# Edge loop of a graph layer: the split of the edge attributes leaves GpSimd for ScalarE and VectorE, and the messages' remainder becomes VectorE's

## The reference

```
x: (1250, 512)   src, dst: (20000,)   edge_attr: (20000, 64)      all float32
edge_feat = concat([x[src], x[dst], edge_attr])        # (20000, 1088)
h         = mish(edge_feat @ W1 + b1)                  # mish(v) = v * tanh(softplus(v))
messages  = mish(h @ W2 + b2)                          # (20000, 512)
agg       = segment_sum(messages, dst)                 # (1250, 512)
u = mish(concat([x, agg]) @ W3 + b3);  y = x + u @ W4 + b4;  layernorm;  then experts
```

## Time and profile before

| | |
|---|---|
| median of 3 runs | 1414.67 us (1414.13 to 1416.09) |
| the profiled execution | 1416.24 us, of it span 1414.6 us |
| busy share of the span | PE 81%, PEld 64%, DVE 78%, ACT 60%, POOL 65% |
| mean granted TensorE clock | 0.933 |
| DMA | 148 MB, mean 105 GB/s |

### The profile page before, as it was taken

One profiled execution on the slowest core, in us unless ns is written; L12 is line 12 of the kernel. 1 busy time (PEld: TensorE's weight loads), 2 busy tenths in 40 slices (PEclk: granted clock), 3 DMA queues, 4 the chain that ended last, 5 costly groups with the idle time before them and its releaser, 6 DMA issues. The chain is left out here.

```text
span 1414.6 us, 20672 instructions
## 1 busy us (share of the span) xinstructions
PE 1145.5 (81%) x5823; PEld 912.1 (64%) x5824; DVE 1108.9 (78%) x1627; ACT 852.9 (60%) x1061; POOL 913.7 (65%) x755
## 2 busy tenths in 40 slices
PE   0992888889889899899898889889838997559972
PEld 0671666777677677677677777767626775558861
DVE  3840579999999999999999999999864876743364
ACT  1311667777777777777777777777843543333341
POOL 1333788898888888889889889888431210454410
PEclk9996899999999999999999999999968997679965
DMA  5534554554554554455455455455210111634452
GB/s 145 200 116 98 117 107 96 109 114 96 107 111 101 102 111 106 98 111 110 98 109 112 96 110 113 96 106 108 81 38 23 37 44 44 189 106 131 127 164 101
DMA packets 113398, 148.00 MB, mean 105 GB/s; under 512 B 55389, under 2 KB 63980, under 8 KB 113225
## 3 DMA queue, kind: packets, MB, share of 16 engines
q0 software_dynamic: 40912, 101.69, 32.8%
q1 hardware_dynamic: 72377, 45.20, 11.6%
q10 hardware_dynamic: 16, 0.02, 0.0%
HBM read 136.29 MB, written 15.66 MB: 107 GB/s over the span
## 5 line engine op out<-in xcount | busy, mean ns | idle before, releaser
L696 POOL DMA_INDIRECT gath<-dst_table,idx_sl x166 | 283.8, 1709 | 49.7 <-issue 27.2
L828 PE MATMUL ps<-W2l,hTh 128*128 128x512 f32 x664 | 264.2, 398 | 0.0
L828 PE MATMUL ps<-W2h,hTh 128*128 128x512 f32 x664 | 263.5, 397 | 0.0
L721 POOL TENSOR_TENSOR msg_lo<-act,msg_hi 128x1024 fp32r<-128x1024 f32 x83 | 213.3, 2570 | 33.9 <-DVE msg_hi L800 33.9
L706 POOL DMA_INDIRECT gath<-src_table,idx_sl x166 | 171.6, 1034 | 76.7 <-issue 50.3
L806 DVE TENSOR_TENSOR dloc<-idx_sl,block_off 128x2 f32<-128x2 int32 x83 | 180.3, 2172 | 14.9 <-DMA idx_sl<-idx_scr 14.9
L828 PE MATMUL ps<-W2h,hTl 128*128 128x512 f32 x664 | 174.9, 405 | 0.4 <-DVE hTl L795 0.2
L828 PEld LDWEIGHTS ps<-W2l,hTh 128*128 128x128 f32 x664 | 125.7, 189 | 30.6
L828 PEld LDWEIGHTS ps<-W2h,hTh 128*128 128x128 f32 x664 | 126.0, 190 | 26.4
L793 DVE TENSOR_TENSOR agg<-agg,ps 125x512 f32 x166 | 112.9, 680 | 31.0 <-DVE agg L793 23.3
L746 ACT ACTIVATE act<-act 128x1024 f32<-128x1024 f32 x83 | 88.2, 1062 | 77.6 <-DVE act L782 77.6
(11 more groups left out here) (315 smaller groups left out, 2852.2 us busy)
## 6 DMA issues: line engine op xcount, KB each, us to landing
f_w_raw<-in_L_ffn_w_dram SPq DMA_DIRECT2D x32, 512.0 KB, 4.6
ea_sl<-ea_scr SPq DMA_DIRECT2D x166, 32.0 KB
ea_scr<-in_edge_attr_dram POOLq DMA_DIRECT2D x1, 5000.0 KB, 20.6
w_raw<-in_L_gnn_W_dram SPq DMA_DIRECT2D x3, 1024.0 KB, 18.6
idx_sl<-idx_scr SPq DMA_DIRECT2D x166, 1.5 KB, 1.7
gath<-src_table,idx_sl POOLq DMA_INDIRECT x166, 4.2
gath<-dst_table,idx_sl POOLq DMA_INDIRECT x166, 5.2
x_raw<-in_x_dram SPq DMA_DIRECT2D x5, 500.0 KB
```

The lines of the kernel that those rows point to most:

```text
L696: pool.indirect_dma_start(out=gath[:, k, j, :], out_offset=None, in_=dst_table[:, :], in_offset=bass.IndirectOffsetOnAxis(ap=idx_sl[:, b % ...
L721: nc.gpsimd.tensor_tensor(msg_lo[:, m % 2], act2[:, m % 3], f32(msg_hi[:, m % 2]), ALU.subtract).then_inc(S["msg_lo_ready"], 1)
L828: return nc.tensor.matmul(ps_2[:, r % 2, j, :], part[:, r % 2, d, j * P:(j + 1) * P], weights[:, d, :], start=False, stop=last)
```

## The change

The attributes are no longer split by POOL. SP loads them twice, into both halves of a tile `ea_sl` that is 128 wide; PE transposes it, so that the 64 attributes stand in PSUM twice, on partitions 0 to 63 and 64 to 127. ACT copies all of it out rounded. A new instruction on DVE then replaces the upper half by what the rounding left (`eaT_lo`, 64 partitions by 256). The messages' remainder `msg_lo` is made by DVE. POOL's loop holds only the gathers.

The order on three engines changes with it. DVE: `hTl`, `msg_hi` and `msg_lo` stand ahead of the additions to `agg`, and `dloc` and `onehot` stand at the end of the step. ACT: the copy of the attributes stands behind both logarithms (it stood between them). PE: four of the eight lo passes stand ahead of the attributes' transposes, and the transposes of `gath` begin with the two blocks that lie in the other PSUM bank.

```diff
-        ea_sl = sb("ea_sl", [P, IN, 2, EDIM])
-        ea_hl = sb("ea_hl", [P, 2, 2, 2 * EDIM], F32R)
+        ea_sl = sb("ea_sl", [P, IN, 2, 2 * EDIM])
...
-                        sp.wait_ge(S["split"], q - IN + 1)
+                        sp.wait_ge(S["eaT_ps"], q - IN + 1)
...
-                        sp.dma_start(ea_sl[:, k, j, :], ea_scr[bass.ds(first, P), :]).then_inc(ea_in[k], 16)
+                        for half in range(2):
+                            sp.dma_start(ea_sl[:, k, j, half * EDIM:(half + 1) * EDIM], ea_scr[bass.ds(first, P), :]).then_inc(ea_in[k], 16)
...
-                    nc.gpsimd.tensor_copy(ea_hl[:, k, :, 0:EDIM], ea_sl[:, b % IN]).then_inc(S["ea_hi"], 1)
-                    pool.wait_ge(S["ea_hi"], b + 1)
-                    nc.gpsimd.tensor_tensor(ea_hl[:, k, :, EDIM:2 * EDIM], ea_sl[:, b % IN], f32(ea_hl[:, k, :, 0:EDIM]), ALU.subtract).then_inc(S["split"], 1)
...
-                    nc.gpsimd.tensor_tensor(msg_lo[:, m % 2], act2[:, m % 3], f32(msg_hi[:, m % 2]), ALU.subtract).then_inc(S["msg_lo_ready"], 1)
...
+                    nc.scalar.activation(a2, a2, ACT.Ln, bias=half_col[:], scale=0.5).then_inc(S["ln2"], 1)
                 if exists(n):
                     act.wait_ge(S["eaT_ps"], n + 1)
...
-                    nc.scalar.activation(eaT[:, n % 2, :], ps_1[:, n % 2, 0, :], ACT.Copy).then_inc(S["eaT_ready"], 1)
-                if second:
-                    act.wait_ge(S["sq2"], g + 1)
-                    nc.scalar.activation(a2, a2, ACT.Ln, bias=half_col[:], scale=0.5).then_inc(S["ln2"], 1)
+                    nc.scalar.activation(eaT[:, n % 2, :], ps_1[:, n % 2, 0, :], ACT.Copy).then_inc(S["eaT_hi"], 1)
...
+                    nc.vector.tensor_copy(msg_hi[:, m % 2], act2[:, m % 3]).then_inc(S["msg_hi_ready"], 1)
+                    dve.wait_ge(S["msg_hi_ready"], m + 1)
+                    nc.vector.tensor_tensor(msg_lo[:, m % 2], act2[:, m % 3], f32(msg_hi[:, m % 2]), ALU.subtract).then_inc(S["msg_lo_ready"], 1)
...
+                t = s + 1
+                if exists(t):
+                    dve.wait_ge(S["eaT_hi"], t + 1)
+                    nc.vector.tensor_tensor(eaT[EDIM:, t % 2, :], ps_1[EDIM:, t % 2, 0, :], f32(eaT[EDIM:, t % 2, :]), ALU.subtract).then_inc(S["eaT_lo"], 1)
...
                     nc.vector.scalar_tensor_tensor(out=act2[:, g % 3], in0=act2[:, g % 3], scalar=1.0, in1=ps_2[:, g % 2],
                                                    op0=ALU.subtract, op1=ALU.mult).then_inc(S["msg_ready"], 1)
+                if exists(n):
+                    dve.wait_ge(*loaded(idx_in, IN, n, 32))
+                    nc.vector.tensor_tensor(dloc[:, 2 * n:2 * n + 2], idx_sl[:, n % IN, :, 2], block_off[:, 2 * n:2 * n + 2], ALU.subtract).then_inc(S["dst_ready"], 1)
+                if exists(m):
+                    dve.wait_ge(S["dst_ready"], m + 1)
+                    nc.vector.tensor_tensor(onehot[:, m % 2], iota_n[:].unsqueeze(1).to_broadcast([P, 2, NE]),
+                                            dloc[:, 2 * m:2 * m + 2].unsqueeze(2).to_broadcast([P, 2, NE]), ALU.is_equal).then_inc(S["onehot_ready"], 1)
...
+                if exists(r):
+                    pe.wait_ge(S["h_lo"], r + 1)
+                    lo_tile(0)
...
-                    pe.wait_ge(S["split"], n + 1)
+                    pe.wait_ge(*loaded(ea_in, IN, n, 64))
...
-                        ins = nc.tensor.transpose(ps_1[:, k, 0, j * P:(j + 1) * P], f32(ea_hl[:, k, j, :]), ident[:])
+                        ins = nc.tensor.transpose(ps_1[:, k, 0, j * P:(j + 1) * P], ea_sl[:, n % IN, j, :], ident[:])
...
+                    lo_tile(1).then_inc(S["lin2_ps"], 1)
...
+                    for d in (2, 3, 0, 1):
+                        if d == 0:
+                            pe.wait_ge(S["eaT_lo"], n + 1)
```

More of the change, by code:

```diff
@@ L648, in edge_phase @@
         src_gath, both_gath = slots("src_gath", GA), slots("both_gath", GA)
-        names = ("ea_hi split dst_ready eaT_ps eaT_ready gath_read lin1_ps exp1 inc1 sq1 ln1 quot1 h_ready h_hi h_lo lin2_ps "
+        names = ("dst_ready eaT_ps eaT_hi eaT_lo gath_read lin1_ps exp1 inc1 sq1 ln1 quot1 h_ready h_hi h_lo lin2_ps "
                  "exp2 inc2 sq2 ln2 quot2 msg_ready msg_hi_ready msg_lo_ready onehot_ready sum_ps summed w3_in w3_hi w3_lo").split()
@@ L752, in _ @@
                     nc.scalar.activation(a1, a1, ACT.Ln, bias=half_col[:], scale=0.5).then_inc(S["ln1"], 1)
+                if second:
+                    act.wait_ge(S["sq2"], g + 1)
+                    nc.scalar.activation(a2, a2, ACT.Ln, bias=half_col[:], scale=0.5).then_inc(S["ln2"], 1)
                 if exists(n):
@@ L785, in _ @@
                     nc.vector.tensor_scalar(act2[:, g % 3], act2[:, g % 3], EXP_MAX, 1.0, ALU.min, ALU.add).then_inc(S["inc2"], 1)
+                if exists(r):
+                    nc.vector.tensor_tensor(hTl[:, r % 2], act1[:, r % 2], f32(hTh[:, r % 2]), ALU.subtract).then_inc(S["h_lo"], 1)
+                if exists(m):
+                    if m >= 2:
+                        dve.wait_ge(S["sum_ps"], m - 1)
+                    dve.wait_ge(S["msg_ready"], m + 1)
+                    nc.vector.tensor_copy(msg_hi[:, m % 2], act2[:, m % 3]).then_inc(S["msg_hi_ready"], 1)
+                    dve.wait_ge(S["msg_hi_ready"], m + 1)
+                    nc.vector.tensor_tensor(msg_lo[:, m % 2], act2[:, m % 3], f32(msg_hi[:, m % 2]), ALU.subtract).then_inc(S["msg_lo_ready"], 1)
                 if exists(a):
@@ L850, in _, with lo_tile @@
                     hi_tile(1)
+                def lo_tile(j):
+                    for d in range(KC):
+                        ins = lin2(j, d, hTl, W2h, d == KC - 1)
+                    return ins
+                if exists(r):
+                    pe.wait_ge(S["h_lo"], r + 1)
+                    lo_tile(0)
                 if exists(n):
                     k = n % 2
-                    pe.wait_ge(S["split"], n + 1)
+                    pe.wait_ge(*loaded(ea_in, IN, n, 64))
                     if n >= 2:
@@ L856, in _ @@
                     if n >= 5:
-                        pe.wait_ge(S["summed"], (n - 4) * 2)
+                        pe.wait_ge(S["summed"], (n - 5) * 2 + 1)
                     for j in range(2):
-                        ins = nc.tensor.transpose(ps_1[:, k, 0, j * P:(j + 1) * P], f32(ea_hl[:, k, j, :]), ident[:])
+                        ins = nc.tensor.transpose(ps_1[:, k, 0, j * P:(j + 1) * P], ea_sl[:, n % IN, j, :], ident[:])
                     ins.then_inc(S["eaT_ps"], 1)
                 if exists(r):
[L862 to L866, removed]
+                    lo_tile(1).then_inc(S["lin2_ps"], 1)
                 if exists(n):
                     k = n % 2
-                    pe.wait_ge(S["eaT_ready"], n + 1)
                     pe.wait_ge(*loaded(both_gath, GA, n, 32))
-                    for d in range(KC):
+                    if n >= 5:
+                        pe.wait_ge(S["summed"], (n - 4) * 2)
+                    for d in (2, 3, 0, 1):
+                        if d == 0:
+                            pe.wait_ge(S["eaT_lo"], n + 1)
                         for j in range(2):
```

10 lines of the change are left out of this document (removed).

## The result

| | before | changed |
|---|---|---|
| median | 1414.40 us | 1568.28 us (1565.02 to 1571.62) |
| ratio | | 1.1085, 95% interval 1.106 to 1.111 |
| profiled execution, span | 1414.6 us | 1565.9 us |
| mean granted clock | 0.933 | 0.879 |

The change costs 154 us.

The account below looks back on a forecast made before the run. Before, POOL and DVE were taken to tie at 10.58 us a pair, the loop of waits 0.2 below. 80 x (13.1 - 10.58) = 202 us on 1416.2, less 1.6 to the median, gave 1616 us; range 1500 to 1655.

Parts of the forecast that it names:

- The path: DVE to PE: `onehot` behind line 818 holds the sum passes and PE's step queued behind them; +1.12 us a pair.
- The signs named for it: DVE's `dloc` 0.15 us, gaps 3 us a pair, `msg_lo` 1.2 us, line 835 waiting 2.4 us; PEclk 0.6 to 0.9.
- The walk: Loop of waits from line 831 to line 831 through PE, ACT and DVE: 11.70 us a pair without a clock fall.
- The bound before: Edge loop before: POOL and DVE tie at 10.58 us a pair, the loop of waits 0.2 us below at 10.37.
- The clock: PE's 2.4 us pause in every pair makes the clock fall in nearly every pair; 1.4 us a pair, period 13.1.
- The first and last steps: The loop's steps outside the 80 full pairs, left as they are in the forecast sum.
- in part of them: Rival on PE's clock: a fall in about every second pair, 1560 us; chance 0.10.
- the one with 0.68: Likeliest outcome on PE's clock: a fall in nearly every pair, 1616 us; chance 0.68.
- The rival built on the rule: PE's clock does not fall, period 11.70, 80 x 1.12 = 90 us more, 1504 us; chance 0.14.
- Relief of DVE: Rival: the period becomes DVE's 9.74 us, 67 us less, 1348 us; chance 0.03.
- the condition named for it: For 1348 us, sum passes must find `onehot` made before PE is through with its step.
- SP and DMA: Two more attribute loads per pair of tiles, 3.4% of the engines; costed at nothing, at most 0.3 us a pair.

Follow-up runs that it names:

- e1: Changed kernel with `dloc` and `onehot` moved ahead of `eaT_lo` and the two mish operations on DVE; 1376.12 us, ratio 0.974.
- e2: Kernel before with only `dloc` and `onehot` moved behind line 818 on DVE; 1592.1 us, ratio 1.1255.
- e6: Kernel before with only the messages' remainder `msg_lo` moved from GpSimd to VectorE, behind `msg_hi`; 1384.83 us, ratio 0.978.
- e4: Changed kernel with all eight lo passes behind the attributes' transposes again; 1406.41 us, ratio 0.994.
- e10: Changed kernel with ACT's copy of `eaT` between the two logarithms again; 1700.3 us.
- e3: Changed kernel with 8 further passes of 512 columns on PE in each step's pause ahead of the sum passes; 1481.95 us, ratio 1.0475.
- e5: Changed kernel with the edits of e1 and e4 joined and the additions to `agg` ahead of `hTl` on DVE; 1359.17 us, ratio 0.960.
- e9: The kernel of e6 with ACT's copy of `eaT` behind the second logarithm; 1347.97 us, ratio 0.947.
- e7: Changed kernel with 2 further passes on PE in each step's pause ahead of the sum passes; 1535.48 us, ratio 1.085.

## Why the prediction was right, and which terms were off

**The path.** The step on which all rested was that `onehot` behind line 818 lies ahead of PE's whole step, and that the sum passes leave the shadow of line 818. Shown by the release of line 835 (158.9 us of waits for `onehot` over the program, none before), by e1, which takes only this away, and by e2, which adds only this. The signs named for it came as well: `dloc` at 0.15 us, `msg_lo` on DVE at 1.23, 3.42 us of gaps on DVE in the pair shown above, the clock at 0.90.

**The walk.** It gave 11.70 for a pair at full clock; measured 11.60. The transposes at 538.34 and the sum pass at 543.78 are 5.44 apart, forecast 5.55. `dloc` to `onehot` is 0.07 and not 0.15. The same walk gave 10.37 for the kernel before without GpSimd's part, and e6 ran at 10.37; started from the measured 11.60, it gave 10.67 for e4 and 12.64 plus a fall for e10. That the copy's move on ACT was used up by the four lo passes is shown by these two: without the first +1.04, without the second -0.93.

**The bound before.** It was a tie of GpSimd and VectorE at 10.58 with the loop of waits 0.2 below. Right: e6 runs at 10.37. I used 10.58 for all pairs, while the mean is 10.68; over 80 pairs this made the forecast loss 8 us too large. For the same reason e6 gained 30 us, more than the 80 x 0.2 of the prediction: the longer pairs went as well.

**The clock.** The mechanism held, the size was too large. A fall costs 13.15 - 11.60 = 1.55 us, where I took 1.4; but it comes in 40 of 55 pairs, where I took nearly every one. Mean 1.13 for 1.4, which is 0.27 x 80 = 22 us. This mis-sized term and the walk's 0.1 (8 us), the 8 us above and the 6 us by which the loop now starts earlier make up 44 of the 48 us. The first and last steps give 8 more: 80 x (12.73 - 10.68) is 164 us, and the stretch between the first and the last sum passes grew by 156.4. Against this stand the 1.0 us behind the loop and 2.6 us by which the medians are further apart (153.9 us) than the two profiled spans (151.3).

Of the outcomes with a chance, the one that came is "in part of them", which had 0.10, and not the one with 0.68. Its time, 1560 for a fall in every second pair, was nearer to 1568 than the point was. The wide range held all three, so that the time lies inside says little about this term. The path and the walk are what the runs bear out.

The rule of the Trainium skill ("TensorE: Matmul & The Clock Gate", section "Why this matters for your kernels"), by which pauses of this length would leave the clock alone, does not hold here. The longest pause of the changed kernel between 250 and 950 us is 2.3 us, and its clock is 0.90; in e3, with the pause filled, it is 1.00. The rival built on the rule, 1504 us, lies nearer to e3 (1482) than to the changed kernel.

**The rivals.** Relief of DVE (1348 us) would have had the right direction in another order of instructions: with the work moved, e1 gains 38 us and e5 56. It failed by the condition named for it; `onehot` was never there in time.

**SP and DMA.** Costed at nothing. The doubled loads bring q1 from 11.6% of the engines' time to 12.0% of a longer span (13.3% of the old one), 1.7 points where 3.4 were forecast, and in the changed kernel POOL waits 2.7 to 4.4 us a pair for PE's reading of `gath`, so the gathers are ahead of PE. e1 has the doubled loads too and is faster than the kernel before.

## What to carry to other kernels

In a hand-written software pipeline, an instruction's place in its engine's order can cost many times its length: ask of each moved instruction which engine's first instruction of the next step waits for it, and what is queued behind that. Walk the loop of waits once around before and after; engine shares did not show it, and here the walk was right to 0.1 us in four kernels (the changed one, e2, e4 and e6). It gives the period only where its loop is the longest: e5 and e9 ran at 10.02 and 9.98 where it gave under 9.5. If TensorE gets a regular pause, price it by the clock as well. Take the pause away if you can (e1, 1376 us); if not, shift independent matmuls into it (e4, 1406 us).

## What was not expected of the hardware

How often the clock fell rises with the length of a pause that comes once in a pair. The share of pairs with a fall, all from 250 to 950 us:

| kernel | pause, us | period without a fall, us | pairs with a fall |
|---|---|---|---|
| e3 | 0.3 | 11.60 | 0 of 60 |
| e4 | 1.38 | 10.67 | 0 of 65 |
| e7 | 1.65 | 11.60 | 27 of 56 |
| changed | 2.31 | 11.60 | 40 of 55 |
| e2 | 2.45 | 11.7 | 43 of 54 |
| e10 | 3.35 | 12.64 (by the walk) | 49 of 49 |

The cleanest comparison is e3, e7 and the changed kernel: the same order of instructions and the same 11.60 us at full clock, with 8, 2 and no passes put into the pause. There 0.3 us of pause gave no fall, 1.65 gave one in half of the pairs, and 2.31 in three of four. e4 has the shorter period as well as the shorter pause, so these runs do not tell which of the two spared it. And e3, with eight passes more in each pair, ran 86 us faster than the changed kernel.
